# DLRM tower: grams in a row with GpSimd's next gathers held back, pairs read by twins of features, the last half through DRAM like the others

## The reference, cut to what matters

```python
# 2048 samples, 27 features of 128 numbers each, one table per feature
e = stack([tbl_f[ids[:, f]] for f in range(27)], axis=1)          # (2048, 27, 128)
interactions = einsum('bfd,bgd->bfg', e, e)                       # 27 x 27 per sample
x = interactions[:, pairs with f > g]                             # 351 per sample
h = concatenate([bottom, x, bottom], axis=1)                      # 128 + 351 + 128
h = maximum(h @ W_top1 + b_top1, 0)                               # 607 -> 512
h = maximum(h @ W_top2 + b_top2, 0)                               # 512 -> 256
y = h @ W_top3                                                    # 256 -> 1
```

## Time and profile before

| | us |
|---|---|
| median of 3 runs | 407.44 (405.29 to 408.83) |
| the profiled execution | 408.56 |
| its span, first to last instruction | 406.8 |
| PE busy | 357.0 (88%) |
| GpSimd busy | 250.9 (62%) |
| DVE busy | 220.1 (54%) |
| ACT busy | 158.7 (39%) |

### The profile page before, as it was taken

How to read it: one execution, slowest core, us unless ns; L and a number is a source line. 1 busy time by engine, 2 the same in 40 slices (tenths; PEclk the granted TensorE clock), 3 DMA queues, 4 the chain that set the end, 5 groups by cost and what they waited for, 6 DMA issues and landing times.

```text
span 406.8 us, 9934 instructions
## 1 busy us (share of the span) xinstructions
PE 357.0 (88%) x3895; PEld 301.1 (74%) x3895; DVE 220.1 (54%) x524; ACT 158.7 (39%) x257; POOL 250.9 (62%) x247
## 2 busy tenths in 40 slices
PE   0770776789699999999999999999999999977997
PEld 0550654678588879889788889799688798876795
DVE  0760687784369984524298983233689835300400
ACT  2321243565224354453334354453243643621533
POOL 5777287677777777777775777777727776000000
PEclk9985799999989999999999999999999999988999
DMA  6999233482655552336454633355445523211100
GB/s 188 232 249 259 72 88 82 134 205 66 160 138 137 127 120 69 86 94 160 138 122 106 138 93 72 83 148 153 112 99 121 127 62 80 53 51 30 24 2 0
DMA packets 60681, 45.55 MB, mean 112 GB/s; under 512 B 31711, under 2 KB 51687, under 8 KB 60635
## 3 DMA queue, kind: packets, MB, share of 16 engines
q1 hardware_dynamic: 51332, 27.39, 28.2%
q0 software_dynamic: 7680, 15.74, 15.8%
q10 hardware_dynamic: 1623, 1.79, 1.8%
HBM read 40.03 MB, written 4.85 MB: 110 GB/s over the span
## 4 chain that ended last, share of the span: by engine, by line
PE 75%; DMA 6%; SPq 6%; DVE 6%; ACT 4%; issue 2%; ACTq 0%
PE ps_build L735 38%; PE ps_dense L782 10%; PE ps_gram L759 9%; PE ps_dense L811 7%; DMA id_raw<-ids_onehot_dram 4%; SPq L296 3%; PE ps_gram L744 3%; ACT embT L569 2%; DVE table L434 2%; PE ps_dense L819 2%; DMA gram_dram<-gram 2%; PE ps_build L744 2%; DVE hot L457 1%; ACT table L558 1%; SPq L297 1%
## 5 line engine op out<-in xcount | busy, mean ns | idle before, releaser
L417 POOL DMA_INDIRECT rows<-tbl_dram,idx x240 | 250.1, 1042 | 92.1 <-issue 69.2
L735 PE MATMUL ps_build<-hot,table 125*128 125x512 f32 x768 | 191.2, 404 | 35.7 <-DVE hot L457 35.1
L735 PEld LDWEIGHTS ps_build<-hot,table 125*128 125x128 f32 x768 | 144.1, 193 | 73.4 <-issue 29.0
L457 DVE TENSOR_SCALAR hot<-id_raw 125x512 fp32r<-125x512 f32 x384 | 154.0, 443 | 55.3 <-PE ps_build L735 51.1
L569 ACT COPY embT<-ps_build 128x512 f32<-128x512 f32 x48 | 57.9, 1207 | 141.3 <-PE ps_build L735 136.2
L759 PE MATMUL ps_gram<-embT 128*53 128x52 f32 x1792 | 48.5, 217 | 4.7 <-DVE gram L465 3.9
L759 PEld LDWEIGHTS ps_gram<-embT 128*53 128x53 f32 x1792 | 46.8, 132 | 7.0 <-issue 5.4
L465 DVE COPY gram<-ps_gram 117x416 f32<-117x416 f32 x28 | 15.5, 587 | 37.6 <-DMA gram_dram<-gram 23.0
L782 PE MATMUL ps_dense<-pairT,w1p 120*128 120x256 f32 (+1 forms) x252 | 35.6, 288 | 0.0
L448 DVE TENSOR_SCALAR id_raw<-id_raw,vocab 125x512 f32<-125x512 int32 x48 | 23.4, 488 | 18.3 <-DMA id_raw<-ids_onehot_dram 18.3
L782 PEld LDWEIGHTS ps_dense<-pairT,w1p 120*128 120x128 f32 (+1 forms) x252 | 33.1, 197 | 0.0
(11 more groups left out here) (61 smaller groups left out, 131.4 us busy)
## 6 DMA issues: line engine op xcount, KB each, us to landing
id_raw<-ids_onehot_dram SPq DMA_DIRECT2D x144, 64.0 KB
raw<-tbl_dram SPq DMA_DIRECT2D x12, 448.0 KB
gram_dram<-gram SPq DMA_DIRECT2D x56, 84.5 KB
rows<-tbl_dram,idx POOLq DMA_INDIRECT x240
id_raw<-ids_onehot_dram SPq DMA_DIRECT2D x12, 256.0 KB
bot<-bottom_dram SPq DMA_DIRECT2D x7, 128.0 KB, 2.4
w1p_raw<-w_pairs_dram ACTq DMA_DIRECT2D x1, 720.0 KB
raw<-tbl_dram SPq DMA_DIRECT2D x12, 52.0 KB
```

Of the source, the lines that this page charges most:

```text
L417: nc.gpsimd.indirect_dma_start(rows[:, t % 2, s * D:(s + 1) * D], None, tables[f], bass.IndirectOffsetOnAxis(idx[:, TILES * i + t, f:f + 1 ...
L457: nc.vector.tensor_scalar(hot[0:VP, a % HOT_SLOTS, :], shifted, float(v), None, ALU.is_equal).then_inc(hot_made, 1)
L735: last = nc.tensor.matmul(bank[:, :], table[0:VP, n, bits, v * D:(v + 1) * D], hot[0:VP, a % HOT_SLOTS, :], start=(v == bits == 0), stop=( ...
```

## The change

Seven things are changed together.

1. `order`: after "rows" (3,0) and (3,1) come gram 0, gram 1, rows (3,2), rows (3,3), gram 2, gram 3, and only then "one" (1,0), "one" (1,1), "two" 1, "three" 1.
2. GpSimd, before it gathers group u = 2 of tile 0 of the next block, waits until all grams of this block are done on PE (`HELD`).
3. The gram is written to DRAM in another layout, with two features (a twin) side by side: each of the four DMAs of a tile has 26 rows of 13 runs of 256 bytes, where it had 26 runs of 3328 bytes.
4. The pairs are read by twins: 18 DMAs for a half in place of 29, still in runs of 128 bytes, and the rows of the weights are put in the same order on the host.
5. Ids are loaded whole (one DMA for a table and block), the three tables that the next block begins with before the gram writes instead of between them; the pacing by gathers is gone.
6. The high and low split of the second half's pairs moves ahead of the grams on ACT and DVE.
7. In the LAST block, grams 2 and 3 are ordinary grams, in two SBUF buffers that alternate (`gram`, `last_gram`), and both of the last two halves go through DRAM. Their dense layers stand in `last_order`, with buffers in the space of the tables. `relayout`, `pairs_back` and the end functions are gone.

```diff
-             ("gram", 0), ("rows", 3, 1), ("rows", 3, 2), ("gram", 1), ("rows", 3, 3), ("one", 1, 0), ("gram", 2),
-             ("one", 1, 1), ("gram", 3), ("two", 1), ("three", 1)]
+             ("rows", 3, 1),
+             ("gram", 0), ("gram", 1), ("rows", 3, 2), ("rows", 3, 3), ("gram", 2), ("gram", 3), ("one", 1, 0),
+             ("one", 1, 1), ("two", 1), ("three", 1)]
+    last_order = order[:order.index(("gram", 3)) + 1] + [
+        ("one", 1, 0), ("one", 1, 1), ("last1", 0, 0), ("two", 1), ("last1", 0, 1), ("three", 1), ("last2", 0), ("last3", 0),
+        ("last1", 1, 0), ("last1", 1, 1), ("last2", 1), ("last3", 1)]
...
+        def gram_free(engine, i, t):
+
+            if is_at(i, LAST) and t == 1:
+                engine.wait_ge(built, BUILDS * LAST + nth("hot", NO - 1) + 1)
+            elif is_at(i, LAST) and t > 1:
+                engine.wait_ge(last_gram_out if t % 2 else gram_out, TILE_OUT * (1 if t % 2 else TILES * i + 1))
+            elif not (is_at(i, FIRST) and t == 0):
+                engine.wait_ge(gram_out, TILE_OUT * (TILES * i + t))
...
-                    src = gram[row:row + PG, k % DUO, :, :].rearrange("p n j -> p (n j)")
-                    sp.dma_start(scratch[t * GROUP + k, :, :, :].rearrange("r n j -> r (n j)"), src).then_inc(gram_out, 16)
+                    src = gram[row:row + PG, k % DUO, :, :].rearrange("p (q n) j -> p q (n j)", n=2)
+                    signal = last_gram_out if is_at(i, LAST) and t % 2 else gram_out
+                    sp.dma_start(scratch[t * GROUP + k, :, :, :, :].rearrange("q r n j -> r q (n j)"),
+                                 src).then_inc(signal, 16)
...
+                src = scratch[half * 2 * GROUP:(half + 1) * 2 * GROUP, :, :, :, :].rearrange("g q r n j -> (q r n) g j")
+                c, p, count, (a, step) = reads[s]
+                rows = src[a:a + (count - 1) * step + 1:step] if step > 1 else src[a:a + count]
+                sp.dma_start(dst[p:p + count, c, :].rearrange("p (g j) -> p g j", j=JT), rows).then_inc(signals[c], 16)
...
+            load_last(0)
+            load_last(1)
+            write_gram(LAST, 0)
+            write_gram(LAST, 1)
             pairs_written(LAST, 0)
             for s in range(READS):
-                read_pairs(0, s)
+                read_pairs(0, s, last_pairX[0], last_pairs_in[0])
+            write_gram(LAST, 2)
+            write_gram(LAST, 3)
+            pairs_written(LAST, 1)
+            for s in range(READS):
+                read_pairs(1, s, last_pairX[1], last_pairs_in[1])
...
                 for u in range(TQ):
                     h, before = (i, t - 2) if t >= 2 else (i - 1, t + 2)
+                    if i > 0 and t == 0 and u == HELD:
+                        pool.wait_ge(grammed[0], GRAMS * i)
+                        pool.wait_ge(grammed[1], GRAMS * i)
...
+                        if is_at(i, LAST) and use[1] == 3:
+                            for c in range(3):
+                                n = CHUNKS[c]
+                                act.wait_ge(last_pairs_in[0][c], 16 * CHUNK_READS[c])
+                                nc.scalar.copy(last_pairT[0][0:n, HIGH, c, :], last_pairX[0][0:n, c, :]).then_inc(last_high, 1)
```

More of the change, by code:

```diff
@@ L32, in slots, with pair_order @@
     return gathered, onehot
+def pair_order():
+    pairs = [(2 * q + 1, 2 * q + 2) for q in range(TWINS)]
+    for q in range(TWINS):
+        pairs += [(r, 2 * q + n + 1) for r in range(2 * q + 1) for n in range(2)]
+    return pairs
 def pair_rows(order):
     rows = []
[L38 to L41, removed]
+    for g, f in pair_order():
+        a, b = max(order[f], order[g]), min(order[f], order[g])
+        rows.append(D + a * (a - 1) // 2 + b)
     return rows
 def pair_reads():
[L47 to L51, removed]
+    first = 2 * PG
+    reads = [(0, 0, TWINS, (3, first + 4))]
+    at = TWINS
+    for q in range(TWINS):
+        n = 2 * (2 * q + 1)
+        cuts = {17: (0, 16, n), 19: (0, 16, n), 21: (0, 16, n), 23: (0, 32, n)}.get(n // 2, (0, n))
         for a, b in zip(cuts, cuts[1:]):
-            reads.append((n, c, at - CHUNK_AT[c] + a, a, b))
+            c = [at < edge for edge in CHUNK_AT[1:]].index(True)
+            assert at + b - a <= CHUNK_AT[c + 1]
+            reads.append((c, at - CHUNK_AT[c], b - a, (q * first + a, 1)))
+            at += b - a
     return reads
@@ L118, in dlrm_tower @@
     READS = len(reads)
-    CHUNK_READS = [len([r for r in reads if r[1] == c]) for c in range(3)]
+    CHUNK_READS = [len([r for r in reads if r[0] == c]) for c in range(3)]
     DENSE = M1 + M2 + 1
-    TAIL = RG + 3
     ctx = ExitStack()
@@ L303, in ids_free @@
                 sp.sem_inc(loads_begun, 1)
+                load_ids(i, n)
             def dense_free(h):
@@ L651, in one_block @@
                             layer3(h)
-                    if is_at(i, LAST) and use == ("one", 1, 1):
-                        act.wait_ge(end_bot_in, 16)
-                        nc.scalar.copy(end_botT[:, HIGH, :], end_bot[:, :]).then_inc(end_bot_high, 1)
+                            if use[1] == 0:
+                                bottom_high(h + 1)
+                                pairs_high(h + 1)
             split_table(0)
@@ L821, in layer3 @@
                 last.then_inc(densed, 1)
-            def relayout():
-                pe.wait_ge(gram_dve, GRAMS * LAST + 2 * TILE_GRAMS + 2)
-                pe.wait_ge(gram_act, GRAMS * LAST + 2 * TILE_GRAMS + 2)
-                for u in range(RG):
-                    bank = end_bank(u)
-                    for n in range(u * RB, min((u + 1) * RB, PG)):
-                        last = nc.tensor.transpose(bank[0:J, (n % RB) * 128:(n % RB) * 128 + GR], gram_end[0:GR, n, :],
-                                                   ident[0:GR, 0:GR])
-                    last.then_inc(end_densed, 1)
@@ L856, in end_layer2 @@
-            def end_layer2():
-                for m in range(M2):
-                    bank = end_bank(TAIL + M1 + m)
-                    for c in range(M1):
-                        if m == 0:
-                            pe.wait_ge(end_h1_made, c + 1)
-                        last = nc.tensor.matmul(bank[:, 0:HALF], w2s[:, c, m * 128:(m + 1) * 128], end_h1[:, c, :],
-                                                start=(c == 0), stop=(c == M1 - 1))
-                    last.then_inc(end_densed, 1)
@@ new lines, in last_layer2, with last_layer3 @@
+            def last_layer2(l, m):
+                bank = last_bank(l, M1 + m)
+                for c in range(M1):
+                    if m == 0:
+                        pe.wait_ge(last_made, DENSE * l + c + 1)
+                    last = nc.tensor.matmul(bank[:, 0:HALF], w2s[:, c, m * 128:(m + 1) * 128], last_h1[l][:, c, :],
+                                            start=(c == 0), stop=(c == M1 - 1))
+                last.then_inc(last_densed, 1)
+            def last_layer3(l):
+                bank = last_bank(l, M1 + M2)
@@ L874, in one_block @@
             def one_block(i, dense):
-                for use in order:
+                for use in last_order if is_at(i, LAST) else order:
                     if use[0] == "hot":
@@ L905, in _ @@
             one_block(LAST, True)
-            relayout()
-            pairs_back()
-            end_layer1()
-            for m in range(M1):
-                layer1(END - 1, m)
-            end_layer2()
-            for m in range(M2):
-                layer2(END - 1, m)
-            end_layer3()
-            layer3(END - 1)
 def kernel(**inputs):
```

375 lines of the change are left out of this document (154 added, 221 removed).

## The result

| | median us | range | ratio to before, 95% interval |
|---|---|---|---|
| before (4 runs) | 408.13 | 405.29 to 412.02 | |
| after (4 runs) | 436.49 | 435.89 to 441.56 | 1.0741 [1.0642, 1.0839] |

The change makes the kernel 28.4 us slower; the forecast was 416.2 with a range up to 426. The profiled execution of after took 441.56 us, 5.1 above its median, with a span of 439.3 where before had 406.8. These are its four stages from the second block on, in the windows view: busy us of PE, PEld, DVE, ACT, POOL, then the granted clock, the DMA share and GB/s.

A forecast was written before the change was run, and what follows sets the result against it. PE was taken to bound the blocks. Blocks 5.7 and 4.5, clock 1.6, FIRST 1.1, rows 0.5, less 4.6 for the tail, sum to 8.8 us slower: 407.4 + 8.8 = 416.2, range 405.5 to 426.

The forecast's parts named there:

- Reads, ids, splits: Fewer pair reads (18 for 29), ids as one DMA and earlier splits: worth nothing in the blocks.
- Grams in a row: Second and third block: PE waits for gram writes and emptyings, losing 5.7 and 4.5 us.
- The formula: In a block, gram 3 starts 5.8 + W0 + W1 after gram 0; the loss is W0 + W1 - 5.1 us.
- W0: Gram 0's write, first DMA issue to next emptying: 5.4 us with gathers; W1, gram 1's: 5.4, or 4.2 quiet.
- Ids as one DMA: Id loads: same bytes, needed 1 us or more after landing, so nothing (up to 1 us if late).
- p: What 256-byte packets add to a gram write's time: 1.0 us, the middle of 0 and 2.0.
- FIRST: First block: gram 3 begins 0.7 us later and the first "hot" units lose 0.4, sum 1.1 slower.
- The tail: From LAST's gram 0 to ACT's last copy: 10.7 us to gain less 6.1 for a new wait, gain 4.6.
- (a): Rival: small packets are free, the hold works as far as it reaches: +0.9 us, 408.3; chance 0.20.
- (c): Rival: each small write costs 34 ns or more, p 2.0 or over: +18.1 us, 425.5; chance 0.15.
- (b): Rival: gram writes quiet throughout, W 3.3, because id pieces, not gathers, disturb them: -6.5 us, 400.9; chance 0.10.
- (d): Rival: held gathers starve PE in the second block by 3 us or more on top: 419 to 420; chance 0.05.

The follow-up runs named there:

- number 1: The changed kernel with the pairs' weights padded to 128 rows (CHUNK = 128 in place of 122); 420.07 us.
- number 5: number 1 with the old gram layout (writes in runs of 3328 bytes, 29 reads a half), ids still whole; 436.32 us.
- number 11: number 1 with grams written in runs of 3328 bytes into the same twin space, so the result is wrong; 418.83 us.
- number 4: number 3 with the old order, grams spread again, in the first three blocks; 413.79 us.
- number 7: number 5 with the old order in the first three blocks, no hold and ACT's split moved behind "one" (1,1), ids whole; 431.77 us.
- number 10: number 6 with the ids in four pieces paced by gathers in place of whole ones; 414.28 us.
- number 8: number 7 with the ids in four pieces, set between the reads and paced by gathers; 406.30 us.
- number 9: number 8 in the twins' layout with its 18 reads a half; 401.52 us.
- number 3: number 1 without GpSimd's hold (its wait for the grams); 422.51 us.
- number 6: number 1 with ACT's split of the last halves' first pairs moved behind "one" (1,1); 415.70 us.
- number 2: The kernel before with CHUNK = 122 in place of 120, nothing else; 422.57 us.

## Why the prediction was wrong, by its steps

**The step that failed** is one that isn't there. "Reads, ids, splits" prices the twin reads, and nothing prices the host side of item 4: `CHUNK = max(CHUNKS)` goes from 120 to 122, and with it the outer dimension of one DMA at the start of the program. It cost 16.4 us in after and 14.3 in the kernel before, by an issue of 12.20 us on ACT's queue that stops ACT for 17.24 and PE for 15.4. The diff had the line, and the trace of before had the load (0.69 us of issue); its price could have been asked for. Without it the measurement is 420.07, and the forecast of 416.2 would have been 3.9 short, inside its range. That it would have come so near is partly luck: the steps below miss in both directions.

**Grams in a row.** The formula is right. From gram 0 in the second block of after, gram 3 should start at 197.13 + 5.8 + 5.94 + 4.93 = 213.8; it starts at 214.17. In the third, 289.7 + 5.8 + 6.39 + 4.34 = 306.2 against 306.32. What was mis-sized is W0: 5.9 to 7.2 in after and number 1 in place of 5.4, by the whole ids, which "Ids as one DMA" put at nothing because it asked only when the ids are needed, not what they delay. p was 0.1 to 0.6, not 1.0, which gave some of it back. The sign that SP's packets rise by some 14 x 1200 missed for the same term: the page has 58648 after 51332, since id loads in one piece take fewer packets (those from 512 bytes to 2 KB fell from 19976 to 1544). The moment up to which GpSimd gathers is 78.6 less 72, 6.6 and not 6.9; nothing turns on it.

**PE standing inside a gram**, 2.66 and 2.55 us, wasn't forecast. Before had it twice, in the narrow grams of LAST (2.50 in the earlier trace rows), and the working filed it under "gone". In after both lie inside W0, so the formula holds in spite of them; only the 0.85 us in gram 3 of the third block are added time. Long runs don't take it away (numbers 5 and 11), spreading the grams or cutting the ids alone only shortens it (1.8 in number 4, 1.9 in number 7, 1.6 and 1.7 in number 10), and with both it is gone (numbers 8 and 9, at most 0.4).

**The blocks' sum** in number 1 is +9.4 and +7.2, where 7.0 and 5.3 were forecast (5.7 and 4.5, 0.8 each for the clock, 0.5 for rows). In the second block W0 and W1 make gram 3 6.8 late, and some 2 more are lost at its start, to two waits for masks (0.55, 0.57) and one stand (0.83). The rows' wait, bounded by 0 to 3, was 2.08 before gram 0 of after, and in number 1 it lies inside W0 and costs nothing. The hold, which the forecast credited with a quiet W1 of 4.2 in the third block, gave 4.3 in after and 4.7 in number 1; what it is worth in all is at most some 2.4 and not clear of noise.

**FIRST.** Forecast +1.1; number 1 starts its second block 1.7 earlier than before. Its W0 and W1 there are 5.7 and 3.3 where 5.4 and 4.2 were counted, and gram 3, which took 4.91 at the lower clock in the kernel before, follows gram 2 without a wait (7.84 for both). Without the hold (number 3) the second block starts 0.8 later than before, so this is near the noise.

**The tail.** Forecast -4.6 for LAST and tail together; number 1 has -4.7 in the tail and +0.8 ahead of it. ACT's wait was put at 4.5 and came at 4.8 (5.1 in after), at the place named. Number 6 takes it away and its tail is 48.3 long, that of number 9 48.0, where 46.0 were counted. This is the part of the change that pays.

**The rivals.** (a), small packets nearly free, was nearly right as a mechanism and wrong as a sum, since W0 grew for another reason. (c) has the nearest time, but not its cause. (b) assumed that id pieces disturb the writes; whole ids disturb them more. (d), the held gathers starving PE, was there with 2.1 us in after, under the 3 or more that it wanted.

With the weights priced, the steps give 416.2 + 14.3 to 16.4 = 430.5 to 432.6, and 0.7 for the median of before, which is 408.13 beside after. The remaining 3 to 5 us are what the blocks lost beyond the forecast: W0, the wait for rows and the stand in gram 3; how much each has isn't separated.

## What to carry to other kernels

Read a diff for every dimension that it alters, also in the host's constants: an outer dimension of a load sets how many engines carry it; 128 rows with zeros were 16 us faster here than 122. Ask of each DMA that is moved what stands behind it on its queue, not only when its own data are due. A wait that is hidden behind other work of the bounding engine is worth more than a tidy order: spreading the grams and dropping the hold was worth 12.4 us with the ids in pieces, 6.3 with whole ones.

## What the hardware showed that I hadn't expected

- An issue that takes 0.45 us took 12.20 (11.84 in number 2) when the load ahead of it ran on few engines, and the compute instructions behind it on ACT stood for 17.24 us. One slow load blocked the engine that issued it.
- PE stood 2.3 to 2.7 us within a stretch of about 250 small matmuls with two instructions each (weights and product), while an instruction packet of 0.02 MB was on its way beside the write and the gathers (one in 200.7 to 203.5 of after). Each of the 16 stands of over 1.5 us with no wait recorded (15 in grams, one in "one"), in eleven of the thirteen profiles, overlaps with such a packet; but a profile has some 28 of these packets (31 at most), and most come with no stand. That the fetch of instructions is the cause is my reading; no run isolates it.
- 256-byte runs written to DRAM cost 0.1 to 0.6 us on 4.5 for 1352 packets. The Trainium skill, in DMA: Bandwidth & Descriptors (Specifications), says that transfers under 512 bytes are read, modified and written. The 2.0 us or more that the prediction put beside this rule don't show here.
